# First W chunk loaded as a gate and an up transfer on two queues, warm-up products on the preamble's zeros, and one mask moved ahead of a W split

## The reference, cut to what matters

```python
gate = lora_add(jnp.einsum('bnh,fh->bnf', x, W_gate), x, A_gate, B_gate)
up = lora_add(jnp.einsum('bnh,fh->bnf', x, W_up), x, A_up, B_up)
act = jax.nn.silu(gate) * up
down = lora_add(jnp.einsum('bnf,hf->bnh', act, W_down), act, A_down, B_down)
...
x = x + ffn(down)        # linear layer with rank-16 adapters and bias
x = x + moe(cond(x))     # masked linear layer, then 64 rank-16 experts, top 16
```

## Time and profile before

| what | value |
|---|---|
| time, median of 3 runs | 355.6 us (355.43 to 355.74) |
| profiled execution, its own time | 355.12 us |
| span of the profiled execution (first to last instruction) | 353.4 us |
| PE busy | 349.5 us (99%) |
| DVE, ACT, POOL busy | 199.6, 143.9, 78.5 us |
| granted TensorE clock, mean over the span | 1.000 |

### The profile page before, as it was taken

How to read it: one execution, slowest core, us unless ns; L and a number is a source line. 1 busy time by engine, 2 the same in 40 slices (tenths; PEclk the granted TensorE clock), 3 DMA queues, 4 the chain that set the end, 5 groups by cost and what they waited for, 6 DMA issues and landing times.

```text
span 353.4 us, 4654 instructions
## 1 busy us (share of the span) xinstructions
PE 349.5 (99%) x1700; PEld 295.3 (84%) x1700; DVE 199.6 (56%) x301; ACT 143.9 (41%) x196; POOL 78.5 (22%) x86
## 2 busy tenths in 40 slices
PE   8999999999999999999999999999999999999996
PEld 7899888888888888888888898888888888888886
DVE  4786655334533453685674565869888867511101
ACT  5666544422442243545464471466352443200100
POOL 2560657863440004000000000000051145002200
DMA  6961343232120053397219019010051022201011
GB/s 223 325 204 43 114 134 116 79 104 75 54 79 0 0 178 125 85 391 291 61 32 305 6 37 416 24 58 5 0 179 60 0 61 60 59 32 59 32 59 59
DMA packets 14803, 37.32 MB, mean 106 GB/s; under 512 B 2273, under 2 KB 4225, under 8 KB 13505
## 3 DMA queue, kind: packets, MB, share of 16 engines
q1 hardware_dynamic: 11920, 31.21, 25.4%
q0 software_dynamic: 2432, 5.57, 5.3%
q10 hardware_dynamic: 432, 0.30, 0.3%
HBM read 34.97 MB, written 2.10 MB: 105 GB/s over the span
## 4 chain that ended last, share of the span: by engine, by line
PE 99%; DVE 0%; issue 0%
PE ps L1153 29%; PE ps L1155 29%; PE ps L1154 29%; PE ps L1175 3%; PE ps L1305 3%; PE ps L1395 1%; PE ps L1382 1%; PE ps L1190 1%; PE ps L1183 1%; PE ps L1194 1%; PE ps L1198 1%; PE ps L1230 1%; PE ps L1404 0%; PE ps L1413 0%; DVE x L1146 0%
## 5 line engine op out<-in xcount | busy, mean ns | idle before, releaser
L1153 PE MATMUL ps<-x_hl,w_hl 128*128 128x512 f32 x144 | 56.1, 390 | 0.0
L1154 PE MATMUL ps<-x_hl,w_hl 128*128 128x512 f32 x144 | 56.1, 390 | 0.0
L1155 PE MATMUL ps<-x_hl,w_hl 128*128 128x512 f32 x144 | 56.0, 389 | 0.0
L460 POOL TENSOR_TENSOR am_hl<-am_raw,am_hl 128x512 fp32r<-128x512 f32 x8 | 11.0, 1387 | 137.7 <-ACT am_hl L477 137.7
L416 POOL DMA_INDIRECT b_raw<-b_gu,row_of x32 | 32.0, 999 | 30.2 <-DVE b_st L778 22.2
L798 DVE TENSOR_TENSOR glu<-glu,ps 128x512 f32<-128x512 f32 (+1 forms) x22 | 14.9, 683 | 39.3 <-ACT glu L509 27.3
L1155 PEld LDWEIGHTS ps<-x_hl,w_hl 128*128 128x128 f32 x144 | 27.0, 188 | 5.7
L509 ACT ACTIVATE glu<-ps 128x512 f32<-128x512 f32 (+1 forms) x22 | 12.8, 589 | 46.3 <-PE ps L1175 46.1
L1153 PEld LDWEIGHTS ps<-x_hl,w_hl 128*128 128x128 f32 x144 | 27.1, 188 | 5.3
L1154 PEld LDWEIGHTS ps<-x_hl,w_hl 128*128 128x128 f32 x144 | 27.1, 188 | 5.2
L1153 PE MATMUL ps<-act,wd_hl 128*128 128x512 f32 x80 | 31.1, 389 | 0.0
(11 more groups left out here) (151 smaller groups left out, 730.8 us busy)
## 6 DMA issues: line engine op xcount, KB each, us to landing
wc_raw<-mask_w SPq DMA_DIRECT2D x8, 1024.0 KB, 7.3
w_raw<-w_gu SPq DMA_DIRECT2D x8, 512.0 KB, 3.2
wd_raw<-w_dn SPq DMA_DIRECT2D x10, 256.0 KB, 2.7
w_raw<-w_t SPq DMA_DIRECT2D x2, 1024.0 KB, 7.1
x<-x_t SPq DMA_DIRECT2D x2, 1024.0 KB, 6.1
am_raw<-a_moe SPq DMA_DIRECT2D x8, 256.0 KB, 2.6
bm_raw<-b_moe SPq DMA_DIRECT2D x4, 512.0 KB, 4.4
x_raw<-x_t SPq DMA_DIRECT2D x7, 256.0 KB, 4.5
```

Of the source, the lines that this page charges most:

```text
L460: nc.gpsimd.tensor_tensor(am_hl[:, j % AM_SLOTS, 1], am_raw[:, j % 2], am_hl[:, j % AM_SLOTS, 0].bitcast(F32), ALU.subtract).then_inc(am_l ...
L1153: nc.tensor.matmul(out, w_high, m_high, start=start, stop=False)
L1154: nc.tensor.matmul(out, w_high, m_low, start=False, stop=False)
L1155: return nc.tensor.matmul(out, w_low, m_high, start=False, stop=stop)
```

## The change

Chunk 0 of tile 0 comes as two transfers: the gate half by ScalarE's queue as its first, the up half by SP as its second, between the two pairs of x. VectorE makes the gate half's high and low parts, ScalarE the up half's high part and VectorE its low part. TensorE's first 12 products are ordered gate first, with new semaphores for the gate's parts. The warm-up products read the zeros that GpSimd writes in the preamble of every program (a constant of one column, repeated), and wait for nothing. VectorE's memset shrinks to 2 columns for ScalarE's use. `t_mask(1)` moves ahead of `w_low(2, 0)`. The numbers of products and of bytes stay the same.

```diff
@@ tiles and semaphores
-        warm = at("warm", [P, P + 1], F32, R_S)
+        warm = at("warm", [P, 2], F32, R_S)
+        dma_up_first, gate_first_hi, gate_first_lo = sem("dma_up_first"), sem("gate_first_hi"), sem("gate_first_lo")
@@ block.sync
             for h in range(2):
                 sp.dma_start(x_raw[:, 0, h * PAIR:h * PAIR + PAIR],
                              x_t[:, 0, h * PAIR:h * PAIR + PAIR]).then_inc(dma_x0_pair[h], 16)
+                if h == 0:
+                    sp.dma_start(w_raw[0][:, 0, 1], w_gu[0, :, 0, 1]).then_inc(dma_up_first, 16)
@@ block.scalar
-            act_e.dma_start(w_raw[0][:, 0], w_gu[0, :, 0]).then_inc(dma_w_first[0][0], 16)
+            act_e.dma_start(w_raw[0][:, 0, 0], w_gu[0, :, 0, 0]).then_inc(dma_w_first[0][0], 16)
...
                 copy(x_hl[:, 0, 0, pair], x_raw[:, 0, pair]).then_inc(x_hi if h else x_pair_hi, 1)
-            act_e.wait_ge(w_hi, 1)
+                if h == 0:
+                    act_e.wait_ge(dma_up_first, 16)
+                    copy(w_hl[0][:, 0, 0, 1], w_raw[0][:, 0, 1]).then_inc(w_hi, 1)
             w_first_high(1, slice(0, 1), 0)
@@ block.vector
             dve.wait_ge(dma_w_first[0][0], 16)
-            nc.vector.tensor_copy(w_hl[0][:, 0, 0:1], w_raw[0][:, 0:1]).then_inc(w_hi, 1)
+            nc.vector.tensor_copy(w_hl[0][:, 0, 0, 0], w_raw[0][:, 0, 0]).then_inc(gate_first_hi, 1)
+            dve.wait_ge(gate_first_hi, 1)
+            low(w_hl[0][:, 1, 0, 0], w_raw[0][:, 0, 0], w_hl[0][:, 0, 0, 0]).then_inc(gate_first_lo, 1)
             for h in range(2):
                 pair = slice(h * PAIR, h * PAIR + PAIR)
                 dve.wait_ge(x_hi if h else x_pair_hi, 1)
                 low(x_hl[:, 1, 0, pair], x_raw[:, 0, pair], x_hl[:, 0, 0, pair]).then_inc(x_lo if h else x_pair_lo, 1)
-                w_first_low(h, slice(0, 1), h + 1)
+                if h == 0:
+                    dve.wait_ge(w_hi, 1)
+                    low(w_hl[0][:, 1, 0, 1], w_raw[0][:, 0, 1], w_hl[0][:, 0, 0, 1]).then_inc(w_lo, 1)
+            w_first_low(1, slice(0, 1), 2)
...
             b_first_low(1)
+            t_mask(1)
             w_low(2, 0)
-            t_mask(1)
             t_low(1)
@@ block.tensor
-            pe.wait_ge(warm_set, 1)
+            zeros = nc.const_aps.tensor(0.0, [P, P], F32)
             for _ in range(WARM_UP):
-                nc.tensor.matmul(ps[:, 7, 0:P], warm[:, 0:P], warm[:, 0:P], start=True, stop=True)
+                nc.tensor.matmul(ps[:, 7, 0:P], zeros, zeros, start=True, stop=True)
...
+            def first_pair(m):
+                pe.wait_ge(w_hi if m else gate_first_hi, 1)
+                pe.wait_ge(x_pair_hi, 1)
+                pair_of(0, m, 0, 0)
+                pe.wait_ge(w_lo if m else gate_first_lo, 1)
+                pair_of(0, m, 1, 0)
+                pe.wait_ge(x_pair_lo, 1)
+                pair_of(0, m, 0, 1)
+
+            def second_pair():
+                pe.wait_ge(x_hi, 1)
+                for m in range(2):
+                    pair_of(1, m, 0, 0)
+                    pair_of(1, m, 1, 0)
+                pe.wait_ge(x_lo, 1)
+                for m in range(2):
+                    pair_of(1, m, 0, 1)
```

More of the change, by code:

```diff
@@ L1223, in adapt_first, with pair_of @@
                         adapt(b_st[1] if f else b_other, FIRST_BANK[n] + m, s)
-            def project_pair(h):
+            def pair_of(h, m, part_w, part_x):
                 pair = slice(h * PAIR, h * PAIR + PAIR)
-                def pass_of(part_w, part_x):
-                    for m in range(2):
-                        nc.tensor.matmul(ps[:, FIRST_BANK[0] + m, pair], w_hl[0][:, part_w, 0, m], x_hl[:, part_x, 0, pair],
-                                         start=h == part_w == part_x == 0, stop=False)
-                pe.wait_ge(w_hi, 1)
-                pe.wait_ge(x_hi if h else x_pair_hi, 1)
-                pass_of(0, 0)
-                pe.wait_ge(x_lo if h else x_pair_lo, 1)
-                pass_of(0, 1)
-                pe.wait_ge(w_lo, 1)
-                pass_of(1, 0)
-            for h in range(2):
-                project_pair(h)
+                nc.tensor.matmul(ps[:, FIRST_BANK[0] + m, pair], w_hl[0][:, part_w, 0, m], x_hl[:, part_x, 0, pair],
+                                 start=h == part_w == part_x == 0, stop=False)
+            def first_pair(m):
[14 more added lines that the diff above has]
+                    pair_of(1, m, 0, 1)
+            for m in range(2):
+                first_pair(m)
+            second_pair()
             project_first(1, 0)
```

2 lines of the change are left out of this document (1 added, 1 removed).

## The result

The changed kernel takes **358.33 us** (median of 6 runs, 356.95 to 359.71), the kernel before in the same session 355.51 us (355.03 to 355.74): ratio 1.0079, interval 1.0062 to 1.0097. It is slower by 2.8 us, and the prediction (355.35, with 0.05 on slower) was wrong. The profiled execution took 357.29 us with a span of 355.6 us, against 355.12 and 353.4 before, so 2.2 us of the loss can be read in the trace.

A forecast was written before the change was run, and what follows sets the result against it. The prediction took PE, busy 349.5 of 353.4 us, as the bound. Stall -0.18, wait -0.06, transfers 0, products and warm-up 0 sum to -0.24 us from 355.6: forecast 355.35 us, range 354.85 to 355.85.

The forecast's parts named there:

- the part on the two transfers: Start-up loads: SP's later issues, 0.43 us late, leave tile 1's chunk landing unchanged and later loads covered; worth 0.
- the mask's 0.18 us: At 39.65 us, PE's stall before the first product with t_st goes: -0.18 us, bounds -0.18 and 0.
- The forecast's own sign of being wrong: Wrong if tile 1's chunk no longer ends the start-up, another stall appears behind 8.3 us, or all products' steps change.
- Rival B: Start-up: the issue's delay passes on, tile 1's chunk lands 0.43 us later; +0.19, so 355.8 us; chance 0.17.
- a chance for tile 1's chunk: Start-up rival: tile 1's chunk lands earlier, ScalarE's queue carrying 64 KB less; -0.62 to -0.72 us; chance 0.15.
- Q: Follow-up theory, not in the prediction: one more issue early in SP's queue makes all later loads late.
- P: Follow-up theory, not in the prediction: the small table lands earlier, and GpSimd's transfers compete with W's.
- Tile 1's first chunk landed as forecast: Start-up: landing taken as unchanged at 5.78 us, bounds 5.0 and 6.2; ScalarE's copy starts at 5.8.
- The three sizes that no row had shown: 128-column parts of tile 0's first chunk: VectorE's cast 0.22, low part 0.29, ScalarE's copy 0.31 us.
- The first product: Start-up: PE's first real product starts at about 4.15 us instead of 4.23.
- the work on the first chunk is worth nothing to the end: Start-up: PE is free 0.34 us earlier, then waits 0.34 us longer for tile 1's W; worth 0.
- rival D: Start-up: the clock stays low after the warm-up, +2.15 us at the front, 357.5 us in all; chance 0.05.

The follow-up runs named there:

- h4: Kernel before plus an unused 2 KB transfer second in SP's queue, GpSimd's first load held until x's second pair is in: 356.73 us, ratio 1.0042.
- h2: Kernel before plus one 2 KB transfer, into a tile nobody reads, as SP's second: 356.99 us, ratio 1.0045.
- e3: The change with the old warm-up and the old order of the mask: 357.97 us, ratio 1.0065.
- f3: Kernel before with the small table moved from ScalarE's queue to SP as its second transfer: 357.04 us, ratio 1.0048.
- f1: The change with GpSimd's first load held until x's second pair is in: 356.07 us, ratio 1.0028.
- g1: Kernel before with ScalarE's first two transfers exchanged, the small table ahead of W's first chunk: 356.75 us, ratio 1.0045.
- e4: The change with GpSimd's gathers held until tile 1's last W transfer is in, its first load still early: 356.31 us, ratio 1.0022.
- g3: The change with GpSimd's first load held for x's second pair and its gathers for tile 1's last W transfer: 356.20 us, ratio 1.0022.
- g2: Kernel before with the small table as SP's second transfer and GpSimd's first load held for x's second pair: 356.30 us, ratio 1.0028.
- f2: The change with the up half on ScalarE's queue, between the gate half and the small table: 355.51 us, ratio 0.9996.
- g4: Kernel before with the mask moved and GpSimd's first load held until tile 0's second W transfer is in: 355.25 us, ratio 0.9991.
- h3: The change with tile 1's first W chunk on ScalarE's queue and GpSimd's first load held for x's second pair: 356.14 us, ratio 1.0023.
- e2: Kernel before with only the second half's mask moved ahead of W's split: 355.15 us, ratio 0.9992.
- e1: Kernel before with only the warm-up on the preamble's zeros and the smaller memset: 355.14 us, ratio 0.9997.
- h1: Kernel before with the mask moved and tile 1's first W chunk on ScalarE's queue instead of SP's: 356.44 us, ratio 1.0031.

## Why the prediction was wrong

**The step that failed** is in the part on the two transfers: "The same holds for the later ones: x chunk 1's low part ends at 7.10 + 0.69 = 7.79, and PE wants it at 8.29, so even 0.43 us passed on stays covered by 0.50." It is what put the transfers into the sum as + 0. Without the mask's 0.18 us they cost 2.4 us in the profiled execution and 3.0 us in the medians. The step took one load behind tile 1's first chunk to speak for all, and took the delay to be at most that of the issue. x chunk 1 did as said: its low part ends at 7.76 in the changed kernel (7.07 + 0.69). But tile 1's last W transfer had a reserve that can be read from before: copy at 10.00, ready at 10.63, PE there at about 11.9. That reserve of 1.3 us would have covered 0.47 nearly three times over. The transfer came 2.81 us later, so the size of the delay is the real error: h4's profile shows 2.51 us for 0.47 us and 2 KB, and its median 1.4 us. The forecast's own sign of being wrong, another stall behind 8.3 us, came true. x's second pair, too, was taken as unchanged (4.72); it was copied at 5.21, which cost nothing here. Rival B had the mechanism (the delay passes on), but at another place and at a price of 0.43 us.

**What was left out** is that the small table lands earlier. I named the 64 KB less in ScalarE's queue only as a chance for tile 1's chunk, and never asked who else waits on that queue. The 64 KB needn't even be the reason: h2 and h4 have all 128 KB there, and the table still lands 2.8 and 2.7 us after its issue. With x's second pair issued at 1.77 it lands 2.5 to 2.8 us after its issue in all ten kernels; with the pair at 1.30 and a W transfer ahead of the table, 3.5 us or more. So one more issue in SP's queue brings both Q and P. GpSimd waits for that table, and its earlier gathers made the second stall: it is in the profiles of the change, e3 and f3 (steps of 0.80 to 2.21 us). Where the gathers are held, or GpSimd starts at 6.5 or later, the longest step there is 0.51 us (f1). An early GpSimd doesn't always bring it: the profiled executions of g1 and h2, both among the fastest of their kernel, are without it. Holding GpSimd back takes the change's loss from 2.8 to between 0.7 and 1.0 us (e4, f1, g3, three intervals below that of the change). In f3 the same hold gives 0.74 us and in h2 0.26, and those intervals overlap, so P's size depends on the kernel around it, and without Q it wasn't measured cleanly (g1).

**The sum as measured**: Q 0.7 to 1.4 us (f1, g2, g3, h4; f1 and g3 have the mask's gain in them, and f1's profile shows its rest at the front and not at W), P in the changed kernel some 2 (e4), the mask -0.18, and 2.8 in all. With f2, where both are absent and the split stays, the time is back at 355.51. One thing doesn't fit: in f2, g4 and h3 W was copied at 11.87 to 12.17, later than in f1 and h2, with SP's issues at their old times and GpSimd's first load at 7.67 or later. f2 and g4 are no slower in the median for it. What makes W late there is open, so a late W copy in one trace isn't the mark of Q; the medians are.

**What held.** Tile 1's first chunk landed as forecast (copy at 5.76 against 5.8). That it agrees so closely is partly luck: with the same start of all queues it was copied between 5.57 (e3, f1) and 6.24 (g3). The mask's gain is 0.18 in the trace. The three sizes that no row had shown were forecast as 0.22, 0.29 and 0.31 us, and the changed kernel's VectorE and ScalarE show:

```profile
3.59 0.23 DVE L830 CAST w_hl<-w_raw 128x128 fp32r<-128x128 f32 x1 [2.60 <-DMA w_raw<-w_gu]
3.85 0.29 DVE L783 TENSOR_TENSOR w_hl<-w_raw,w_hl 128x128 fp32r<-128x128 f32 x1
...
3.77 0.31 ACT L480 ACTIVATE w_hl<-w_raw 128x128 fp32r<-128x128 f32 x1
```

The first product came at 3.95 (4.15 forecast), since x's first pair was copied at 3.39 instead of 3.67. That the work on the first chunk is worth nothing to the end is borne out by f2, which has it whole and gains nothing: tile 1's first product starts there at 6.40, behind the copy of its W.

**The front and rival D.** Tile 1's first product came at 7.03, not 6.27. The last six of the 12 products started at 5.68 (timeline of PE, 6.0 to 7.5 us, changed kernel):

```profile
5.68 1.51 PE L1237 MATMUL ps<-x_hl,w_hl 128*128 128x256 f32 x6
```

Six steps later PE was at 7.03: 0.23 us each on average, although nothing was waited for any more (x's low part was ready at 6.08). That is about the 0.24 of the level of 1.2 GHz, though the granted clock of the stretch reads 1.00. That looks like D. But the old warm-up shows the same in e2, and the zeros don't in e1 (timelines of PE, e2 first):

```profile
4.26 2.79 PE L1230 MATMUL ps<-x_hl,w_hl 128*128 128x256 f32 x12
6.88 0.62 PE L1190 MATMUL ps<-x_hl,w_hl 128*128 128x512 f32 x2
```

```profile
4.21 2.34 PE L1230 MATMUL ps<-x_hl,w_hl 128*128 128x256 f32 x12
6.39 0.71 PE L1190 MATMUL ps<-x_hl,w_hl 128*128 128x512 f32 x2
```

So the moment at which the level of 2.4 GHz comes differs by about 0.5 us between executions, with either warm-up. The Trainium skill ("TensorE: Matmul & The Clock Gate", Part 1) says that this moment varies by ±500 ns; these traces, one execution of each kernel, agree. In the changed kernel these 0.7 us cost nothing, since PE would have waited until 13.49 in any case. Where no later stall takes them up they count, as in f1's profile. How much of the medians that makes up wasn't measured.

## What to carry to other kernels

When a start-up is bound by loads, count every transfer that is issued ahead of others: read for each later load its landing and when it is wanted, down to the last one before the queue drains, and don't price a later issue at its own 0.43 us. For everything that lands earlier, ask who waits for it and what that engine will issue. Here the split in halves was free on the queue that carried the whole (f2) and cost 2.8 us with one half on the other. And read several executions before a landing is blamed: one trace can miss the loss of the median (h2) or show a stall that the median doesn't (g4).

## What the runs showed of the hardware

- One more transfer of 2 KB as the second of SP's queue cost 1.4 us (h4, 1.0042), three times the 0.47 us by which the later ones were issued later. It also brought the small table, on another queue, 0.9 us earlier (2.7 instead of 3.6 us after its issue). The rate from 5 to 9 us was 254 to 278 GB/s in all nine kernels with that shift, and 280 to 331 in the eight others and before. Why issues that are 0.47 us later go with a lower rate for so long is **open**. The rate doesn't decide alone (f2: 280 GB/s at 355.51 us), and a late issue without any additional transfer wasn't tried.
- The time of issue alone doesn't set the landing: tile 1's chunk, issued at the same time on ScalarE's queue, was copied 1.48 us later (h1). The Trainium skill ("DMA: Bandwidth & Descriptors", "Queues, rings and completion order") says that each DMA engine takes turns between the queues that have work; h1 is in line with it, and so are GpSimd's gathers that hold up SP's loads (e4), but no run here shows the turns themselves. The prediction used that page's rule that a second queue only saves issue time. By the turns, the share of a queue changes too, which the prediction passed over.
- The same page's rule ("Rules for kernel authors") that transfers under 64 KB are mostly overhead isn't tested by the halves, which are 64 KB: with two of them on one queue the kernel takes the time of the kernel before within the measurement (f2, 0.9980 to 1.0012).
